# Selective scan: two products move from GpSimd to VectorE, and the states are summed by token

## What is computed

```python
A = -jnp.exp(A_log)
dA = Delta[..., None] * A
A_bar = jnp.exp(dA)
B_bar = jnp.expm1(dA) / (dA + 1e-06) * Delta[..., None] * B_proj[:, :, None, :]
def step(h, inp):
    a_t, b_t, c_t, u_t = inp
    h = a_t * h + b_t * u_t[..., None]
    y_t = jnp.sum(h * c_t[:, None, :], axis=-1)
    return (h, y_t)
...
out = y * _silu(gate) @ W_out + residual
```

## Time and profile before

| | us |
|---|---|
| median of three runs | 5262.86 (5252.82 to 5270.24) |
| the profiled execution | 5278.73 |
| its span, first to last instruction | 5277.1 |
| in it, the scan: first to last reciprocal | 690.8 to 1931.3 |

### The profile page before, as it was taken

The page is one execution under the profiler, slowest core; times in us unless marked ns, Lnnn a source line. Parts: engine busy times, 40 slices in busy tenths (PEclk is TensorE's granted clock), DMA queues, the critical chain, the costliest instruction groups (busy, mean ns, idle before and its releaser), DMA issues. The chain is left out here.

```text
span 5277.1 us, 87603 instructions
## 1 busy us (share of the span) xinstructions
PE 3710.5 (70%) x29867; PEld 2711.8 (51%) x29867; DVE 3465.9 (66%) x4350; ACT 2548.1 (48%) x4148; POOL 2620.2 (50%) x1660
## 2 busy tenths in 40 slices
PE   2996735545555549966925988899989889894594
PEld 1663334445444446655812555566655555564483
DVE  6882567777777768850045888888878788885101
ACT  1222455556565642222201766667766677684221
POOL 0220389999999972212021666665556566600202
PEclk9998866666777769968956999999999999996697
DMA  2000000000000000024522222222222222202254
GB/s 82 0 0 11 0 26 26 28 26 28 26 28 26 28 34 0 0 70 136 186 76 65 55 52 51 53 52 67 46 63 50 48 54 54 53 12 88 76 188 128
DMA packets 237298, 276.33 MB, mean 52 GB/s; under 512 B 63771, under 2 KB 185556, under 8 KB 235536
## 3 DMA queue, kind: packets, MB, share of 16 engines
q1 hardware_dynamic: 224032, 244.85, 17.0%
q0 software_dynamic: 8704, 24.35, 1.4%
q10 hardware_dynamic: 4224, 2.76, 0.2%
HBM read 152.60 MB, written 36.04 MB: 36 GB/s over the span
## 5 line engine op out<-in xcount | busy, mean ns | idle before, releaser
L2169 DVE TENSOR_TENSOR att_b_prob_low<-att_b_prob,att_b_prob_high 128x1024 f16<-128x1024 f32 (+2 forms) x640 | 768.2, 1200 | 190.3 <-ACT att_b_prob_high L2130 158.8
L2136 ACT ACTIVATE att_b_prob<-att_b_score,att_soft 128x1024 f32<-128x1024 f32 (+2 forms) x640 | 631.1, 986 | 197.8 <-PE att_b_score L2041 123.6
L2196 DVE TENSOR_REDUCE att_b_neg_max<-att_b_peek 128x1 f32<-128x1024 f32 (+1 forms) x748 | 667.7, 906 | 69.5 <-PE att_b_peek L2018 51.9
L1023 PE MATMUL mix_scan_hT<-ident,mix_scan_h 128*128 128x128 f32 x1024 | 259.3, 403 | 598.6 <-DVE mix_scan_h L972 583.7
L960 DVE RECIPROCAL mix_scan_inv<-mix_scan_inv 128x512 f32<-128x512 f32 x128 | 429.2, 3353 | 366.1 <-POOL mix_scan_inv L843 366.1
L2130 ACT CAST att_b_prob_high<-att_b_prob 128x1024 f16<-128x1024 f32 (+2 forms) x640 | 588.1, 919 | 33.6 <-PE att_b_o L2069 16.1
L2065 PE MATMUL att_b_o<-att_b_vh,att_b_prob_high 128*128 128x65 f16 x4352 | 463.1, 195 | 94.2 <-DVE att_b_heads L2187 55.8
L1023 PEld LDWEIGHTS mix_scan_hT<-ident,mix_scan_h 128*128 128x128 f32 x1024 | 189.9, 212 | 632.1 <-DVE mix_scan_h L972 526.7
L2065 PEld LDWEIGHTS att_b_o<-att_b_vh,att_b_prob_high 128*128 128x128 f16 x4352 | 399.2, 98 | 218.0 <-DVE att_b_prob_low L2169 128.1
L2067 PE MATMUL att_b_o<-att_b_vl,att_b_prob_high 128*128 128x64 f16 x4352 | 460.8, 193 | 0.0
L2069 PE MATMUL att_b_o<-att_b_vh,att_b_prob_low 128*128 128x65 f16 x4352 | 460.5, 194 | 0.0
(11 more groups left out here) (336 smaller groups left out, 9565.7 us busy)
## 6 DMA issues: line engine op xcount, KB each, us to landing
moe_w<-in_L_ffn_W_dram SPq DMA_DIRECT2D x64, 1024.0 KB, 8.1
mix_scan_b_row<-mix_b_rows SPq DMA_DIRECT2D x128, 256.0 KB, 3.2
att_b_crossed<-att_b_raw SPq DMA_DIRECT2D x512, 64.0 KB, 2.0
att_b_q_both<-att_b_halves SPq DMA_DIRECT2D x240, 64.0 KB, 2.0
att_b_k_twice<-att_b_halves SPq DMA_DIRECT2D x240, 64.0 KB, 2.0
moe_slots_in<-moe_route_zero SPq DMA_DIRECT2D x2, 4096.0 KB, 14.9
...
```

Source lines behind the costliest of these rows:

```text
L1023: last = pe.transpose(hT_ps[:, j * D + m * P:j * D + (m + 1) * P], hs[:, b * W + m * GRP + t * P:b * W + m * GRP + (t + 1) * P], ident[:, :])
L2136: act.activation(prob[:, at:at + width], score[m % 2][:, 0:width], ACT.Exp, scale=soft[:, 0:1])\
L2169: dve.tensor_tensor(prob_low[:, at:at + width], prob[:, at:at + width], prob_high[:, at:at + width], ALU.subtract).then_inc(low_ready, 1)
L2196: last = dve.tensor_reduce(neg_max[:, first + col:first + col + 1], peek_bank(kind, s)[:, base:base + nb * P], AX.X, ALU.max, negate=True)
```

## The change

GpSimd gives up the pair product and the B row product; VectorE takes the first just ahead of the reciprocal and the second behind (a+1)*tanh. GpSimd's `inputs` (the product den*du) is written two units ahead, behind `dub`, and waits for `den` itself. ScalarE's `den` waits for the pair product too. y is now summed token-major (identity stationary, hcT moving, two matmuls of 256 columns for each half where four of 128 were), so it has to be turned: ScalarE copies it out of PSUM (`copy_y`), TensorE transposes it channel half by channel half into out_ps (`turn_y`), and VectorE gates each half from there. The product with w_out, `keep_two` and the last addition move two units later. The diff, cut to its core:

```diff
@@ @block.gpsimd
-            prime(pool, *[row_used] * AHEAD, *[den_used] * AHEAD, *[tanh_used] * AHEAD)
+            prime(pool, *[den_used] * AHEAD, *[tanh_used] * AHEAD)
...
-            def pair(u, b):
+
+            def inputs(u, b, g):
                 wait_apart(pool, den_ready, u + 1, (set_up, SETS))
-                pool.tensor_tensor(inv[:, b * GRP:(b + 1) * GRP], cols(den, b, 0), cols(den, b, 1), ALU.mult)\
-                    .then_inc(pair_ready, 1)
...
+                if not (isinstance(u, int) and u < AHEAD):
+                    wait_apart(pool, input_ready, u - 1, (set_up, SETS))
                 pool.tensor_tensor(both(cols(factor, b)), both(cols(den, b)),
...
                     pool.tensor_tensor(cols(factor, b), cols(factor, b), cols(tanh, b), ALU.mult).then_inc(tanh_used, 1)
-                    if more:
-                        pair(unit + 1, 1 - b)
-                    wait_apart(pool, inverse_ready, unit + 1, (set_up, SETS))
-                    wait_apart(pool, b_landed[b], (g * (S_N // 2) + n // 2 + 1) * 16, (set_up, SETS))
+                    wait_apart(pool, row_used, AHEAD + unit + 1, (set_up, SETS))
+                    wait_apart(pool, tanh_used, AHEAD + unit + 1, (set_up, SETS))
+                    wait_apart(pool, scanned, (unit + 1) * KD, (set_up, SETS))
...
-                    if more:
-                        inputs(unit + 1, 1 - b, at)
+                    if n + AHEAD < S_N:
+                        inputs(unit + AHEAD, b, g)
+                    elif not last:
+                        inputs(unit + AHEAD, b, g + 1)
@@ @block.scalar
+                    wait_apart(act, pair_ready, unit + 1, (set_up, SETS))
...
-                    if n in (3, 5) and not first:
-                        keep_two(g - 1, (n - 3) // 2)
+                    if n == 1 and not first:
+                        copy_y(g - 1)
+                    if n in (5, 7) and not first:
+                        keep_two(g - 1, (n - 5) // 2)
+
+            def copy_y(g):
+
+                for half in range(HALVES):
+                    act.wait_ge(summed, g * S_N * HALVES + (S_N - 1) * HALVES + half + 1 + PRIMED)
+                    if half == 0:
+                        wait_unless_first(act, y_turned, g * KD)
+                    act.copy(yT[:, half * (W // HALVES):(half + 1) * (W // HALVES)], yT_ps[half][:, :]).then_inc(y_copied, 1)
@@ @block.vector
-            def factors(u, b):
+            def factors(u, b, landed):
...
-                dve.wait_ge(pair_ready, u + 1)
+                dve.wait_ge(den_ready, u + 1)
+                wait_unless_first(dve, input_ready, u - 1)
+                dve.tensor_tensor(one, cols(den, b, 0), cols(den, b, 1), ALU.mult).then_inc(pair_ready, 1)
+                dve.wait_ge(pair_ready, AHEAD + u + 1)
                 dve.reciprocal(one, one).then_inc(inverse_ready, 1)
...
+                dve.wait_ge(b_landed[b], landed * 16)
+                dve.wait_ge(inverse_ready, u + 1)
+                dve.tensor_tensor(one, one, b_row[:, b * GRP:(b + 1) * GRP], ALU.mult).then_inc(row_used, 1)
...
+            def gated(g, m):
+
+                dve.wait_ge(y_turned, g * KD + m + 1)
+                if m == 0:
+                    wait_unless_first(dve, out_ready, g * 2)
+                dve.tensor_tensor(cols(yg, 0, m), out_ps[:, :], gate[:, bass.ds(g * GRP + m * TOK, GRP)], ALU.mult)\
+                    .then_inc(yg_ready, 1)
...
-                        if n == 1:
-                            gated(g - 1)
-                        elif n in (3, 5):
-                            add_out(g - 1, (n - 3) // 2)
+                        if n in (1, 2):
+                            gated(g - 1, n - 1)
+                        elif n in (5, 7):
+                            add_out(g - 1, (n - 5) // 2)
@@ @block.tensor
+                    last = pe.matmul(yT_ps[half][:, j * D:(j + 1) * D], ident[:, :],
+                                     hcT[:, b * W + t * D:b * W + (t + 1) * D],
+                                     start=(n == 0 and j == 0), stop=(n == S_N - 1), skip_group_check=True)
...
+            def turn_y(g, m):
+
+                if m == 0:
+                    pe.wait_ge(y_copied, (g + 1) * HALVES)
+                    pe.wait_ge(added, PRIMED + g * GT)
+                else:
+                    pe.wait_ge(yg_ready, g * KD + m)
+                for t in range(GT):
+                    last = pe.transpose(out_ps[:, t * P:(t + 1) * P], yT[:, t * D + m * P:t * D + (m + 1) * P], ident[:, :])
+                last.then_inc(y_turned, 1)
...
-                    if n in (2, 4) and not first:
-                        out(g - 1, (n - 2) // 2)
+                    if n in (1, 2) and not first:
+                        turn_y(g - 1, n - 1)
+                    if n in (4, 6) and not first:
+                        out(g - 1, (n - 4) // 2)
```

More of the change, by code:

```diff
@@ L849, in inputs @@
                     .then_inc(den_used, 1)
-            pair(0, 0)
-            inputs(0, 0, 0)
+            for n in range(AHEAD):
+                inputs(n, n, 0)
             def body(g, first, last):
@@ L856, in body @@
                     b, unit = n % 2, g * S_N + n
-                    more = not (last and n == S_N - 1)
-                    at = g if n + 1 < S_N else g + 1
                     wait_apart(pool, expm1_ready, unit + 1, (set_up, SETS))
@@ L936, in _ @@
                 take(NG - 1, n)
+            copy_y(NG - 1)
             for part in range(2):
@@ L941, in _ @@
         def _(dve):
-            prime(dve, *[scanned] * (AHEAD * KD), added)
+            prime(dve, *[scanned] * (AHEAD * KD), *[row_used] * AHEAD, *[pair_ready] * AHEAD, added)
             dve.memset(eps[:, :], EPS_BAR)
@@ L973, in recur @@
                                            state[:, at:at + 1], ALU.mult, ALU.add).then_inc(scanned, 1)
-            def gated(g):
-                dve.wait_ge(summed, (g + 1) * S_N * HALVES + PRIMED)
-                for m in range(KD):
-                    done = dve.tensor_tensor(cols(yg, 0, m), y_ps[m][:, :],
-                                             gate[:, bass.ds(g * GRP + m * TOK, GRP)], ALU.mult)
-                done.then_inc(yg_ready, 1)
+            def gated(g, m):
[4 more added lines that the diff above has]
+                    .then_inc(yg_ready, 1)
             def add_out(g, part):
@@ L995, in body @@
                     if not (last and n == S_N - 1):
-                        factors(unit + 1, 1 - b)
+                        factors(unit + 1, 1 - b, g * (S_N // 2) + (n + 1) // 2 + 1)
                     recur(unit, b, n)
                     if not first:
-                        if n == 1:
-                            gated(g - 1)
-                        elif n in (3, 5):
-                            add_out(g - 1, (n - 3) // 2)
-            factors(0, 0)
+                        if n in (1, 2):
+                            gated(g - 1, n - 1)
+                        elif n in (5, 7):
+                            add_out(g - 1, (n - 5) // 2)
+            factors(0, 0, 1)
             turns(dve, body)
-            gated(NG - 1)
+            for m in range(KD):
+                gated(NG - 1, m)
             for part in range(2):
@@ L1054, in body @@
                     if n > 0:
-                        sum_half(g, n - 1, 1, not first)
+                        sum_half(g, n - 1, 1)
                     elif not first:
-                        sum_half(g - 1, S_N - 1, 1, True)
+                        sum_half(g - 1, S_N - 1, 1)
                     turn_half(unit, b, 1)
-                    sum_half(g, n, 0, not first)
-                    if n in (2, 4) and not first:
-                        out(g - 1, (n - 2) // 2)
+                    sum_half(g, n, 0)
+                    if n in (1, 2) and not first:
+                        turn_y(g - 1, n - 1)
+                    if n in (4, 6) and not first:
+                        out(g - 1, (n - 4) // 2)
             turns(pe, body)
-            sum_half(NG - 1, S_N - 1, 1, True)
+            sum_half(NG - 1, S_N - 1, 1)
+            for m in range(KD):
+                turn_y(NG - 1, m)
             for part in range(2):
```

25 lines of the change are left out of this document (8 added, 17 removed).

## The result

The changed kernel takes 5346.35 us (median of four runs, 5334.55 to 5349.71) where the kernel before took 5265.3 on the same chip (four runs): a ratio of 1.0146 on record, 95% interval 1.013 to 1.0163 (the two medians alone give 1.0154). It is slower by 81 us, and the time forecast was 5347. The profiled execution took 5345.28 us, its span 5343.7. All of the loss lies in the scan: from the first reciprocal to the last it took 1240.5 us before and takes 1312.3 now; the rest of the program takes some 5 us less than in the profiled execution of before.

What follows compares the result with a forecast made beforehand. GpSimd was taken to bound the scan. Ordinary units -50, group starts +124, keep_two +7 and the end +3 gave +84 us: profiled execution 5278.7 to 5363, median 5347. The range was 5215 to 5400 us.

Steps and rivals of the forecast that it cites:

- GpSimd bounds, and VectorE would need 8.05 a unit with no collision: Scan unit: GpSimd takes 9.59 us, VectorE 6.71; with both products moved VectorE takes 8.05, alone a 220 us gain.
- Exclusion of whole products, the earlier start wins, a waiter goes before the next: VectorE products with two SBUF inputs and GpSimd's SBUF products wait each other out whole; a waiter precedes the next product.
- The rival without it: Scan's products do not exclude each other; late `den` still holds units to 8.2 us; about 5210 us, chance 0.06.
- The ordinary unit, 9.3 us: Scan units away from group starts: 9.3 us, ends 9.0 and 9.5; 107 units at -0.47 give -50 us.
- one calm unit in seven: Assumed share of ordinary units where the pair product gets in before GpSimd's product with tanh, at 8.40 us each.
- `dub` starts 0.14 after F: On GpSimd in each unit, `dub` begins 0.14 us after the end of the product with tanh (F).
- the second rival: `dub` beats the pair product, a margin of 0.07 us; each unit stays at 11.52 us; 5584 us, chance 0.10.
- The start of a group, 47.0 us for three units: Three new waits for the turned y at seven group starts: 47.0 us for 29.3, +124 us, ends 92 and 138.
- S0 to S1: From the end of a group's first unit's scans to the end of its second's: put at 15.8 us.
- the fast case: After a group's second unit, fast TensorE lets the pair product in first: 13.3 us instead of 16.6; 15.6 was taken.
- The copy: ScalarE's copy of y from PSUM at a group's start: 0.84 us as an upper bound.
- Small terms: keep_two delaying `den` in two units per group, +7 us; copy, turns and gates at the scan's end (tail), +3.

Runs made afterwards that it cites:

- the PSUM operand: The changed kernel with the second operand of VectorE's pair and row products read from PSUM, so values differ from the reference's: 5216.09 us, ratio 0.9909.
- `den` first: ScalarE computes the next unit's `den` ahead of `take`: on the changed kernel 5237.94 us, with gates also later 5149.76, with only the two products moved 5125.97.

## Why the prediction was right

The time came out at 5346.35 for a forecast of 5347.0, which is closer than its terms were. By its own steps:

- *GpSimd bounds, and VectorE would need 8.05 a unit with no collision*: right. With the PSUM operand the unit is 8.00.
- *Exclusion of whole products, the earlier start wins, a waiter goes before the next*: right, shown by the rows at 1292.37 and 1301.29 and by the operand from PSUM. The rival without it is out (its own sum, -66 to -20, has its middle at 5220 and not at the 5210 stated).
- *The ordinary unit, 9.3 us*: the round was forecast scan to scan as 8.05, 8.75, 11.52. The scans of the round shown end at 1284.44, 1292.45, 1301.37 and 1312.87: 8.01, 8.92, 11.50. Beside this round there are eleven units of 10.1 to 10.2 us that the working did not have. The mean over the 106 ordinary units is 9.40. My allowance of one calm unit in seven was too large: calm stretches lie almost only in the first group, units of 8.29 to 8.55. Worth: -39 us, with keep_two's share in it, where -50 and +7 were put.
- *Within it, `dub` starts 0.14 after F*: wrong, it is 0.31. I took the gap from the row of F behind the `den` product, another pair of instructions with other waits. This made the pair's lead over `dub` larger than the 0.07 on which the second rival (5584) hung, and the row product's wait 0.35 (1.04 us) and not 0.21.
- *The start of a group, 47.0 us for three units*: 45.1 measured. S0 to S1 was put at 15.8 and is 15.58. For the next two the working had 16.6, or 13.3 with TensorE fast, and I took 15.6. Both cases occur: 16.6 twice in groups 1 and 7, about 14.0 in groups 2 to 6, where the pair is wanted 5.7 to 6.1 us behind the scans (S1+6.11 in the rows above) and not at 5.2, as the 13.3 supposed. The 15.6 weighs the fast case at a third; it came in five groups of seven. Worth: +111 us where +124 was put.
- *The copy*: 0.585 us, within the 0.84 bound.
- *Small terms*, +10: keep_two's 7 are inside the ordinary mean and were not measured apart. The tail's 3 did not show: from the last reciprocal to the scan's last instruction it is 25.9 us for 27.4 before.
- The sum: the stage grew by -39 + 111 = +72 us, against -50 + 124 + 7 = +81. The profiled executions differ by 67 us, the medians on one chip by 81: the profiled run of before stood above its median, as the prediction noted, and that of after did not. The mechanism was right and both large terms were near, but the agreement to 1 us is luck: the ordinary units gained 4 us less than was put, the starts lost 13 less, and the pair of profiles from which these terms are read differs from the pair of medians by 14.

What the prediction did not see is in the experiments: a gate or an addition written between the scans and the pair product can cost a wait for a whole GpSimd product. With `den` first such a unit is 10.7 us for 8.3, the 0.7 to 1.3 us of the operation included; written behind the pair product, the same operations save 25 us at 21 places. In the changed kernel this is hidden among the other long units.

Left open: what sets TensorE's clock in groups 1 and 7 apart from the others, and what makes a stage ahead of the scan faster when `den` is written first; no run took them up.

## What to carry to other kernels

Before moving work between VectorE and GpSimd, count VectorE instructions with two SBUF inputs; each can wait for a whole GpSimd product, so either give one operand a place in PSUM (the kernels here that do it compute other values; none was built that keeps the reference's) or write the instruction where it is issued at once while GpSimd is between products. When the bound moves, look at the inputs that were late but had slack: here one ScalarE operation written earlier was worth 2.2 to 2.6% (0.9927 against 1.0146, 0.9757 against 1.0021, 0.9705 against 0.9944), of which 11 to 15 us, 0.2 to 0.3%, lie ahead of the scan. A result that crosses three engines needs slack at each crossing: here a unit or two took the waits at the starts away.

## What the runs showed of the chip

- Two engines' SBUF products exclude each other for the whole instruction, in both directions, and the wait is booked as busy time of the one that waits: VectorE's 0.66 us product takes up to 2.88, GpSimd's 2.35 up to 2.92. In the rows shown above a GpSimd product that VectorE was ahead of takes 2.58 to 2.80.
- With one operand in PSUM products of this shape are 0.66 to 0.69 us in all 255 cases.
- The gap between two GpSimd products in a row is not one number: 0.17 us ahead of the `den` product, 0.31 ahead of `dub`, in the kernel before 0.14 ahead of the product with tanh. That it is the number of waits in between is likely, not shown. It decides who goes first.
- A ScalarE copy of 512 fp32 columns out of PSUM took 0.585 us, two scaled copies of 256 columns 0.84.
